# One compare on 16-bit numbers for the narrow one-hots of eight meetings, in the count matrix's build of a four-layer graph network

## The reference, cut to what matters

```
agg = jax.ops.segment_sum(x[src], dst, num_segments=N_NODES)      # GIN
mean = agg / jnp.maximum(cnt, 1.0)[:, None]                       # SAGE, three times
return mean @ W_l.T + x @ W_r.T + b
```

## Time and profile before

| | us |
|---|---|
| median of three runs | 9359.47 |
| lowest, highest | 9359.37, 9371.02 |
| span of the profiled execution | 9364.4 |
| the build of the count matrix in it | 2301 to 3464 |
| of that, while `bucketed` is read back | 2301 to 2655 |
| VectorE busy in the whole span | 5660.6 (60%) |
| TensorE matmul busy in the whole span | 7028.5 (75%) |
| ScalarE busy in the whole span | 2515.7 (27%) |

### The profile page before, as it was taken

How to read it: one execution, slowest core, us unless ns; L and a number is a source line. 1 busy time by engine, 2 the same in 40 slices (tenths; PEclk the granted TensorE clock), 3 DMA queues, 4 the chain that set the end, 5 groups by cost and what they waited for, 6 DMA issues and landing times. The chain is left out here.

```text
span 9364.4 us, 133857 instructions
## 1 busy us (share of the span) xinstructions
PE 7028.5 (75%) x35740; PEld 4596.9 (49%) x35792; DVE 5660.6 (60%) x16783; ACT 2515.7 (27%) x5863; POOL 2656.2 (28%) x2952
## 2 busy tenths in 40 slices
PE   4777777775566659940488699999998777777787
PEld 4555555453122224420477544444445666666676
DVE  6777777775589990059899800000014777777786
ACT  0222222222467740020388600000001333310001
POOL 0777777776470000000000000000002444444410
PEclk9767776766679989975799899999999999999998
DMA  3333333334975538849566478787886766642363
GB/s 99 103 103 105 105 104 103 105 105 167 393 231 164 168 114 306 299 195 426 205 215 216 144 262 276 262 287 256 295 284 200 181 180 179 179 111 63 63 178 88
DMA packets 969628, 1759.77 MB, mean 188 GB/s; under 512 B 102288, under 2 KB 665125, under 8 KB 905315
## 3 DMA queue, kind: packets, MB, share of 16 engines
q1 hardware_dynamic: 683820, 1335.73, 44.1%
q0 software_dynamic: 110720, 276.01, 9.0%
q10 hardware_dynamic: 174394, 139.51, 5.5%
HBM read 1412.04 MB, written 338.80 MB: 187 GB/s over the span
## 5 line engine op out<-in xcount | busy, mean ns | idle before, releaser
L768 POOL DMA_INDIRECT bucketed<-arena,wide x1563 | 1515.6, 970 | 726.5 <-issue 714.0
L1920 PE MATMUL psum<-wide,arena 128*128 x6496 | 1209.9, 329 | 400.5 <-DVE arena L1979 393.9
L1920 PEld LDWEIGHTS psum<-wide,arena 128*128 128x128 f32 x6496 | 989.9, 195 | 618.3 <-issue 493.3
L1787 POOL DMA_DIRECT2D table<-wide x13 | 9.7, 743 | 4316.2 <-DVE wide L1711 4316.2
L1979 DVE TENSOR_SCALAR arena<-wide,tile_first 128x128 f32 x3248 | 870.8, 300 | 472.3 <-PE psum L1920 293.8
L1841 POOL DMA_INDIRECT arena<-table,src_i x832 | 803.3, 966 | 1009.1 <-PE psum L1937 872.4
L1660 PE MATMUL psum<-arena,h 128*128 128x512 f32 (+1 forms) x2548 | 1048.6, 570 | 19.1 <-DMA arena<-adjacency 17.5
L922 PE MATMUL psum<-arena 128*128 128x512 bf16 x2253 | 695.7, 442 | 435.0 <-DVE arena L870 259.4
L665 PE MATMUL psum<-arena 128*113 128x177 bf16 x1568 | 534.4, 341 | 416.2 <-ACT wide L687 374.6
L870 DVE TENSOR_SCALAR arena<-sums 128x512 bf16<-128x512 int16 x2304 | 799.9, 347 | 0.0
L659 PE MATMUL psum<-w_edge,arena 128*128 128x256 f32 x1568 | 786.9, 597 | 0.0
(11 more groups left out here) (398 smaller groups left out, 11006.0 us busy)
## 6 DMA issues: line engine op xcount, KB each, us to landing
arena<-adjacency SPq DMA_DIRECT2D x294, 1024.0 KB
arena<-adjacency SPq DMA_DIRECT2D x98, 1568.0 KB, 7.8
adjacency<-wide SPq DMA_DIRECT2D x588, 256.0 KB
arena<-adjacency SPq DMA_DIRECT2D x196, 640.0 KB, 3.9
arena<-adjacency SPq DMA_DIRECT2D x147, 768.0 KB
arena<-bucketed POOLq DMA_DIRECT2D x208, 528.0 KB, 6.0
arena<-adjacency SPq DMA_DIRECT2D x49, 1792.0 KB, 6.9
arena<-adjacency SPq DMA_DIRECT2D x49, 1344.0 KB, 6.1
```

Source lines behind the costliest of these rows:

```text
L768: e.indirect_dma_start(bucketed, bass.IndirectOffsetOnAxis(ap=places[k][0:size, c:c + 1], axis=0), rows[k][0:size, c, :], None).then_inc(s ...
L1920: e.matmul(flat[:, ds((chunk & 3) * 512 + 2048, P)], lhsT=hot[:, i % 8, :], rhs=table_in[:, ds(tile * P, P)], start=False, stop=True, skip ...
```

## The change

The buffer of narrow one-hots is cut into two halves of eight meetings each, laid out as 4 pairs of meetings by 128 columns by 2 meetings, so that the two meetings of a pair lie side by side. The row numbers `row_of` are kept as int16 instead of float32, and a table `pairs_from_one` holds each of the numbers 1 to 128 twice. One tensor-tensor compare of 1,024 elements then makes eight narrow one-hots. It is issued in front of the first and of the ninth meeting of a run. The wait in front of it asks for eight free slots instead of four. The wide one-hots stay as they are. TensorE reads its 128 weights at a step of two elements.

```
-            hot_src = room(RUN * P // 2).bitcast(bf16).rearrange("p (k n) -> p k n", k=RUN)
+            hot_src = [room(RUN // 2 * P // 2).bitcast(bf16).rearrange("p (j n k) -> p j n k", j=RUN // 4, k=2) for _ in range(2)]
...
-            key_of, row_of = (part(sums, 512 + HITS * k, HITS) for k in range(2))
+            pairs_from_one = part(sums, 256, P).bitcast(i16).rearrange("p (n k) -> p n k", k=2)
+            key_of = part(sums, 512, HITS)
+            row_of = part(sums, 512 + HITS, HITS // 2).bitcast(i16).rearrange("p (j k) -> p j k", k=2)
...
-                        e.tensor_copy(row_of[:, b * P:(b + 1) * P], psum[:, 5, P:2 * P]).then_inc(s_rows, 1)
+                        e.tensor_copy(row_of[:, b * HALF:(b + 1) * HALF, :], psum[:, 5, P:2 * P].rearrange("p (j k) -> p j k", k=2)).then_inc(s_rows, 1)
...
                                 if k % BANKS == 0:
-                                    e.wait_ge(s_used, i * RUN + k + BANKS)
-                                e.tensor_scalar(hot_src[:, k, :], from_one[:, 0:P], row_of[:, ds(i * RUN + k, 1)], None, op0=ALU.is_equal)
+                                    e.wait_ge(s_used, i * RUN + k + 2 * BANKS if k % (RUN // 2) == 0 else i * RUN + k + BANKS)
+                                if k % (RUN // 2) == 0:
+                                    at = (i * RUN + k) // 2
+                                    e.tensor_tensor(hot_src[k * 2 // RUN], pairs_from_one.unsqueeze(1).broadcast_to([P, RUN // 4, P, 2]),
+                                                    row_of[:, at:at + RUN // 4, :].unsqueeze(2).broadcast_to([P, RUN // 4, P, 2]), ALU.is_equal)
                                 e.tensor_scalar(hot_key[:, k, :], from_one[:, 0:GROUP * P], key_of[:, ds(i * RUN + k, 1)],
                                                 None, op0=ALU.is_equal).then_inc(s_ready, 1)
...
                     e.wait_ge(s_one, 1)
+                    e.tensor_copy(pairs_from_one, from_one[:, 0:P].unsqueeze(2).broadcast_to([P, P, 2])).then_inc(s_one, 1)
+                    e.wait_ge(s_one, 2)
                     take(0)
...
-                                e.matmul(flat[:, ds((bucket[k] & (BANKS - 1)) * 512, 512)], lhsT=hot_src[:, k, :], rhs=hot_key[:, k, :],
+                                e.matmul(flat[:, ds((bucket[k] & (BANKS - 1)) * 512, 512)], lhsT=hot_src[k * 2 // RUN][:, k % (RUN // 2) // 2, :, k % 2], rhs=hot_key[:, k, :],
```

## The result

The changed kernel takes 9307.38 us, the median of four runs between 9301.73 and 9310.45; the kernel before, beside it on the same chip, 9362.70 us (9359.37 to 9371.02, four runs). The ratio is 0.9935, with a 95% interval of 0.9923 to 0.9947: **about 0.65% faster, 55 to 61 us**. The profiled execution took 9310.45 us with a span of 9308.7, against the span of 9364.4 before.

What follows compares the result with a forecast made beforehand. VectorE was taken to bound the build's middle stretch, with ScalarE capping the gain. 50 us there plus 9 in the padding make 59 off the 9364.4 span, 9305.4; the median stands 4.9 lower, so 9300 us, range 9272 to 9345.

Steps and rivals of the forecast that it cites:

- likeliest case: Whole kernel: the forecast of 9300 us, its own range 9272 to 9318, chance 0.63.
- Middle stretch: Build from 2655 to 3409 us, VectorE busy 753.5 of 754 us: gain 50 us, bounds 20 and 81.
- Padding: Build from 3409 to 3464 us: eight runs go from 6.80 us to 5.6, gain 9 us, bounds 3 and 11.
- First stretch and the other edits: Build from 2301 to 2655 us, DMA engines full, and the waits, doubled table, int16 copy, strided weights: counted at zero.
- The new compare: VectorE's 1,024-element compare at two elements at a time: lasts 695 ns, occupies 0.60 us, replacing eight narrow ones of 1.32 us.
- ScalarE's cap: Middle stretch: ScalarE's row of 13 blocks takes 17.5 us at least, capping the gain at 72 to 81 us.
- TensorE's own run: Middle stretch: a TensorE run unstarved by VectorE takes 5.6 us, 0.352 per meeting.
- One at a time: Rival: VectorE's new compare runs one element at a time, 1.13 us; total 9323 us, chance 0.13.
- Strided weights: Rival: TensorE's weight loads at a step of two are not hidden, making the kernel slower; 9394 us, chance 0.06.
- Nothing: Rival: the change does nothing since the middle stretch was ScalarE's all along; 9359 us, chance 0.05.
- The handover: Rival: TensorE's loads, in series with bank waits, become the bound and coarser slots add stalls; 9345 us, chance 0.13.
- VectorE's 154 us: Middle stretch: gain if VectorE alone set the time, its need falling from 0.442 to 0.352 us per meeting.

Runs made afterwards that it cites:

- meetings outermost: Guarded changed kernel, its eight-meeting compare with columns innermost, row number one repeated element instead of a pair, weights packed: 10388.73 us, 0.4242 us per meeting.
- short clear: Guarded changed kernel with ScalarE clearing 64 of a bank's 512 columns, counts wrong: 10428.55 and 10395.97 us, 0.432 us per meeting.
- the `and`: One extra register operation (and with 4095) on the value in every wait against a loaded number; added to the kernel before: 10350.82 us, ratio 1.0087.
- guarded changed kernel: Changed kernel plus the `and` in every wait on a loaded number: 10396.76 and 10384.10 us, ratios 1.0112 and 1.0110 to the plain kernel before.

## Why the prediction was right

**Total and parts.** 9300 was forecast, 9307.38 came, within the likeliest case's own range. Middle stretch: 50 forecast, 48.8 measured. Padding: 9 forecast, 11.6 measured. First stretch and the other edits: 0 forecast, 354 us both times.

**The new compare** was worked out from L710 and L361 as 695 ns, occupying 0.60 us. It is 687 to 702 ns and 0.60 us. The step that int16 in and bf16 out keep the rate of two elements holds, and the run with meetings outermost shows that it is the pairs and not the batch of eight. The run with compares of 512 elements confirms the split as well: 689 ns for 1,024 and 421 for 512 make 1.05 ns per pair and 153 ns fixed, where 1.02 and 175 were taken. By the formula of the Trainium skill (VectorE: DVE Perf Modes, the section on the TRN2 errata) VectorE would have gained 35 us in the stretch. The stretch alone became 49 us shorter, with VectorE waiting 85 us in it. The formula was near for the new compare, 594 ns against 600 of occupancy, and far off for the eight it replaces, 94 ns each against 165.

**ScalarE's cap** gave the right number, and that is in good part luck. A row of 13 was to take 17.5 us at least; 497 blocks in 705.2 us are 38.2 rows of 18.4 us. But the engine that fills most of the time is not ScalarE: TensorE's own queue takes 478 of the 560 us, and 57 more pass between its groups, most of them in waits for banks. The row head is part of those waits, since taking its register load away wins 5.4%. Whether the 13 x 1.14 of copying belongs to them is not decided: short clear takes nearly 5 us off each row and wins 15 ns per meeting between groups, but lengthens TensorE's register loads and wins nothing in sum. I took two thirds of the cap; the fraction was chosen, not shown, and no run confirms it.

**TensorE's own run** came out right for the middle stretch by two errors that cancel. The prediction put it at 5.6 us, 0.352 per meeting; the steps give 5.54 us. In the changed kernel's timeline, where look-ups and transposes don't intervene:

```profile
2926.90 4.19 PE L929 MATMUL psum<-arena 128*128 128x512 bf16 x16 [1.14 <-DVE arena L875]
2932.95 4.35 PE L929 MATMUL psum<-arena 128*128 128x512 bf16 x16 [1.87 <-DVE arena L875]
2938.54 1.07 PE L929 MATMUL psum<-arena 128*128 128x512 bf16 x4 [1.24 <-DVE arena L875]
```

Runs start 6.05 and 5.59 us apart, 0.378 and 0.349 per meeting. The idle time at their heads is put down to VectorE, but all three start 0.35 to 0.36 us after the register load has ended. That load (L922 in the changed kernel) is not one number:

```profile
L922 PEldq TENSOR_LOAD <-wide x86: 1102/1566/2330, 2811.7 to 3364.2; - x86
```

```profile
L922 PEldq TENSOR_LOAD <-wide x7: 1102/1103/1107, 3369.9 to 3401.9; - x7
```

The first is the stretch with stores running, 1.57 us in the median and up to 2.33; the second the padding, 1.10 us. The prediction's 2.17 us from a last group to the next run came from the padding of the kernel before: a group of 1.07 and the short register load of 1.10. In the middle stretch the same step is 3 x 0.217 + 1.97 = 2.62 us. Against that, a group whose inputs are ready takes 3 x 0.217 + 0.322 = 0.97 us and not 1.15 (3372.41 to 3373.38 above). For the padding the errors don't cancel: TensorE alone takes 3 x 0.97 + 2.17 = 5.1 us there, which is the step from 3371.41 to 3376.53, and VectorE with 5.40 is the slower. The padding brought 12 us and not 9.

A pause costs more than its length. ScalarE at a row head, TensorE's wait for its bank, and what TensorE and VectorE do then:

```profile
3102.27 0.59 ACT L955 COPY wide<-psum 128x512 f32<-128x512 f32 x1 [2.67 <-issue]
...
3103.71 8.52 PE L929 MATMUL psum<-arena 128*128 128x512 bf16 x24 [2.48 <-ACT psum L957]
...
3104.96 0.15 PEld L929 LDWEIGHTS psum<-arena 128*128 128x128 bf16 x1 [0.28 <-issue]
...
3105.39 0.15 PEld L929 LDWEIGHTS psum<-arena 128*128 128x128 bf16 x1 [0.28 <-issue]
3105.63 0.69 DVE L873 TENSOR_TENSOR arena<-sums 128x1024 bf16<-128x1024 int16 x1 [3.56 <-PE psum L929]
```

Weight loads come 0.43 us apart there, and last 0.15 us, where a group at the full clock has steps of 0.22 us and 0.097 per load. TensorE has come back from its pause at the lower of its two levels, and VectorE waits 3.56 us. The prediction held the clock at its mean of 0.92, which is what it stayed. In this pause the low part falls just behind it, when TensorE should catch up; but steps at the low level cost the changed kernel no more than the kernel before.

**The rivals.** One at a time: falls (702 ns, not 1216). Strided weights: falls (97 against 96 ns; a group of four still lasts 1.07 us, as in the earlier trace rows). Nothing: falls with the result. The handover: its mechanism, TensorE's register loads in series with its waits for banks, is the one that the steps show; its price was wrong. It was to leave the pace just under the old one, 0.44; the pace went to 0.41. With ScalarE's row heads gone it stays at 0.39, not 0.352. Of VectorE's 154 us in the middle stretch 49 came out.

**The signs named ahead**: compare 695 (702), ScalarE's idle time about 120 and mostly row heads (132.6, of which 108.2 is put down to TensorE), VectorE waiting for TensorE (84.4), stretch 700 (705.2), padding runs 5.6 (5.1 to 5.5), clock 0.92 (0.92).

## What to carry to other kernels

A two-input compare on 16-bit numbers took 0.69 us for 1,024 elements with adjacent pairs innermost in both inputs and in the output, and 1.22 us with one input repeated element by element; a table with each number twice buys that, and TensorE reads the result at a step of two for a nanosecond per load. When the engine that was full is relieved, count the others' queues too: with register loads at the heads of runs TensorE needed 0.346 us per meeting of its own, and with its waits for banks two thirds of VectorE's saving did not come out. An idle time in front of an instruction is named after the last semaphore; set it beside the end of the register load before blaming an engine. And look at what the relieved engine had been slowing: the same edit that wins 0.65% on one chip won nothing in total on another, with the `and` in both kernels there, because of the stretch where GpSimd issues its stores.

## What the runs showed of the hardware that was not expected

- Register loads from SBUF are of very different length: 16 values on TensorE's queue 1.10 us in the padding, 1.57 us in the median while 256 KB stores run, and over 2.5 us in 24 of 81 cases with the short clear; what lengthens them was not tested. Others in the median: 13 values on ScalarE's queue 3.14 us, on GpSimd's 3.8 us; one value on GpSimd's 0.43 us.
- GpSimd's issue of a small indirect store lasts 1.39 us beside VectorE's stream of narrow compares and 0.94 us without it. On chip 7, in the guarded changed kernel, a register operation on TensorE's queue took 700 ns in the median instead of 32 while the shorter issues followed each other; on the first chip the shorter issues came without that.
- One more `and` in front of a wait made the smallest step between TensorE's groups 0.093 us longer, though such an operation is recorded with 32 ns.
- Making the clear of a bank shorter made the kernel slower (0.432 against 0.416 us per meeting, twice). The register loads on TensorE's queue were longer with it; why is open.
- With products of 128 columns instead of 512, at nearly the same pace, TensorE's granted clock was 0.51 over 560 us, against 0.94 with 512 columns.
